# An equivariant 2-to-2 layer whose sums, line terms and slope are placed on other engines, and streaming matmuls placed between the steps of a window attention

## The reference, cut to what matters

```python
diag = jnp.diagonal(x, axis1=-2, axis2=-1)
sum_diag = jnp.sum(diag, axis=-1, keepdims=True)
sum_rows = jnp.sum(x, axis=-1); sum_cols = jnp.sum(x, axis=-2)
sum_all = jnp.sum(sum_rows, axis=-1, keepdims=True)
ops = [diag[..., :, None] * eye, sum_diag[..., None] * eye, sum_rows[..., :, None] * eye, sum_cols[..., :, None] * eye,
       sum_all[..., None] * eye, bt(sum_cols[..., None, :]), bt(sum_rows[..., None, :]), bt(sum_cols[..., :, None]),
       bt(sum_rows[..., :, None]), x, jnp.swapaxes(x, -1, -2), bt(diag[..., :, None]), bt(diag[..., None, :]),
       bt(sum_diag[..., None]), bt(sum_all[..., None])]
```

## Time and profile before

| | us |
|---|---|
| three runs | 975.45, 972.47, 974.67 (median 974.67) |
| profiled execution, its own time | 975.6 |
| its span, first to last instruction | 973.8 |
| mean granted TensorE clock | 0.974 |
| busy: PE, DVE, ACT, POOL | 889.0, 414.4, 446.7, 239.2 |
| 1024 dependent steps of L2 (L927, L950), from about 410 to 897 | 487 |

### The profile page before, as it was taken

How to read it: one execution, slowest core, us unless ns; L and a number is a source line. 1 busy time by engine, 2 the same in 40 slices (tenths; PEclk the granted TensorE clock), 3 DMA queues, 4 the chain that set the end, 5 groups by cost and what they waited for, 6 DMA issues and landing times. The chain is left out here.

```text
span 973.8 us, 15415 instructions
## 1 busy us (share of the span) xinstructions
PE 889.0 (91%) x6191; PEld 518.6 (53%) x6272; DVE 414.4 (43%) x714; ACT 446.7 (46%) x1498; POOL 239.2 (25%) x144
## 2 busy tenths in 40 slices
PE   8778889888989888899999999999999999999887
PEld 5336667767845444344444444455555544554543
DVE  5699999999966753500000000002005400202763
ACT  5777777776636531333333333333333333334641
POOL 4149999998910000300000000000000000000410
PEclk9989999999999996999999999999999999999987
DMA  3110000000000000200000000000000000000000
GB/s 82 23 43 2 1 1 1 1 1 1 1 7 1 1 25 11 83 1 1 1 1 1 1 1 1 1 1 1 1 1 1 1 1 1 1 1 2 1 25 11
DMA packets 10220, 8.30 MB, mean 9 GB/s; under 512 B 7246, under 2 KB 8510, under 8 KB 10052
## 3 DMA queue, kind: packets, MB, share of 16 engines
q1 hardware_dynamic: 10148, 7.31, 3.1%
HBM read 5.47 MB, written 0.26 MB: 6 GB/s over the span
## 5 line engine op out<-in xcount | busy, mean ns | idle before, releaser
L908 PE MATMUL L2p_z<-stream 128*128 128x512 bf16 x880 | 342.2, 390 | 0.0
L950 ACT ACTIVATE L2yx<-L2p_z 32x2 f32<-32x2 f32 x1024 | 165.3, 161 | 323.0 <-PE L2p_z L927 323.0
L927 PEld LDWEIGHTS L2p_z<-L2yx,L2v 64*32 64x32 f32 x2048 | 137.6, 104 | 224.7 <-ACT L2yx L950 218.5
L927 PE MATMUL L2p_z<-L2yx,L2v 64*32 64x2 f32 x2048 | 225.5, 178 | 16.9 <-ACT L2yx L950 15.9
L788 POOL TENSOR_TENSOR hc<-hs,cb 128x1024 f32<-128x1024 f32 x64 | 149.6, 2363 | 4.4 <-DVE hs L729 4.4
L558 PEld LDWEIGHTS p_y<-ident,hc 128*128 128x128 f32 x1024 | 123.2, 192 | 16.5 <-POOL hc L788 9.1
L1641 DVE COPY xn_one<-L2yx 32x512 f32<-32x512 f32 (+1 forms) x2 | 0.8, 384 | 302.7 <-ACT L2yx L950 302.7
L558 PE MATMUL p_y<-ident,hc 128*128 128x128 f32 x1024 | 125.4, 276 | 4.3 <-POOL hc L788 4.3
L1641 POOL COPY xn_one<-L2yx 32x128 f32<-32x128 f32 x1 | 0.3, 284 | 484.2 <-SPq L1984 484.2
L729 DVE TENSOR_TENSOR_SCAN hs<-d_a,p_bb 128x1024 f32<-128x1024 f32 x48 | 109.8, 2287 | 6.2
L908 PEld LDWEIGHTS L2p_z<-stream 128*128 128x128 bf16 x943 | 90.1, 96 | 15.1
(11 more groups left out here) (522 smaller groups left out, 898.2 us busy)
## 6 DMA issues: line engine op xcount, KB each, us to landing
y_l<-in_pick SPq DMA_DIRECT2D x1, 768.0 KB
b_parts<-part SPq DMA_DIRECT2D x6, 128.0 KB, 2.3
c_parts<-part SPq DMA_DIRECT2D x6, 128.0 KB, 2.4
pos<-in_pos SPq DMA_DIRECT2D x1, 512.0 KB, 3.6
ao<-in_at_o SPq DMA_DIRECT2D x1, 512.0 KB, 4.0
L1w<-in_L_w SPq DMA_DIRECT2D x1, 297.0 KB
L3w<-in_L_w SPq DMA_DIRECT2D x1, 297.0 KB
above<-in_x SPq DMA_DIRECT2D x2, 128.0 KB, 3.1
```

The costliest lines, as they stand in the source:

```text
L908: pe.matmul(p_z[:, 1, 0:each], stream[:, 0:128], stream[:, 0:each], start=True, stop=True)
L927: pe.matmul(p_step[:, t % 2], v[:, 0:C], yx[:, NB * t:NB * (t + 1)], start=True, stop=True).then_inc(s("preact"), 1)
L950: act.activation(yx[0:C, NB * (t + 1):NB * (t + 2)], p_step[:, t % 2], ACT.Sigmoid).then_inc(s("state"), 1)
```

## The change

In the equivariant stage a table `esum` (128 tokens x 8 x 98 columns: 32 row indicators, 32 column indicators, 32 diagonal indicators, one for the whole diagonal and one of ones) is loaded as a third DMA. Eight float32 matmuls of `xn_tok` by `esum` give all sums in PSUM, and VectorE copies them to `sums`. The biases enter as a sixth term of the lines. The lines are copied to `rc` by VectorE and ScalarE, and TensorE adds them to the product by identity matmuls whose moving operand is a broadcast of `rc`. Matrix 10 moves behind the lines and is followed by two streaming matmuls. The slope is split: ScalarE writes 0.99 x relu to `positive`, VectorE adds 0.01 of the product to `x` and then `positive`. At the stage's end stand 12 streaming matmuls in place of 17. In the attention, 4 streaming matmuls are placed ahead of `sum_squares`, 2 instead of 1 behind it, and 5, 2, 2 and 1 in the last part, the 5 behind a wait for the last maxima.

```diff
...
@@ -1388,92 +1388,99 @@
     experts("L1", 0)
 
 
+    NSUM = 3 * SIDE + 2
     with ExitStack() as st:
         ew = sb("ew", [R, NBASIS, R], stack=st)
         eb = sb("eb", [R, 2], stack=st)
-        sr = sb("sr", [R, SIDE], stack=st)
-        scl = sb("scl", [R, SIDE], stack=st)
-        dg = sb("dg", [R, SIDE], stack=st)
-        tot = sb("tot", [R, 2], stack=st)
+        esum = sb("esum", [128, T // 128, NSUM], stack=st)
+        sums = sb("sums", [R, NSUM], stack=st)
+        sr, scl, dg = (sums[:, k * SIDE:(k + 1) * SIDE] for k in range(3))
+        sd, sa = (sums[:, 3 * SIDE + k:3 * SIDE + k + 1].broadcast_to([R, SIDE]) for k in range(2))
         rc = sb("rc", [R, 3, SIDE], stack=st)
-        acc = sb("eacc", [R, SIDE, SIDE], stack=st)
-        low = sb("elow", [R, SIDE, SIDE], stack=st)
+        positive = sb("epos", [R, T], stack=st)
+        SLOPE = 0.01
         p_a = ps("e2p_a", [128, T], stack=st)
         p_b = ps("e2p_b", [128, T], stack=st)
         p_c = ps("e2p_c", [128, 2, BANK], stack=st)
         p_r = ps("e2p_r", [128, 2, BANK], stack=st)
+        p_s = p_a[0:R, 0:NSUM]
-        xi = xn[:].rearrange("p (i j) -> p i j", j=SIDE)
         with nc.Block() as block:
             @block.sync
             def _(sp):
                 sp.dma_start(ew[:], io["eq_w"]).then_inc(sig["load_eq"], 16)
                 sp.dma_start(eb[:], io["eq_b"]).then_inc(sig["load_eq"], 16)
-                sp.wait_ge(sig["load_eq"], 32)
+                sp.dma_start(esum[:], io["eq_sum"]).then_inc(sig["load_eq"], 16)
+                sp.wait_ge(sig["load_eq"], 48)
 
             @block.tensor
             def _(pe):
                 norm.pe(pe, 6)
-                pe.wait_ge(sig["load_eq"], 32)
-                norm.wait_out(pe)
+                pe.wait_ge(sig["load_eq"], 48)
+                for j in range(T // 128):
+                    last = pe.matmul(p_s, xn_tok[:, j], esum[:, j], start=(j == 0), stop=(j == T // 128 - 1))
+                last.then_inc(sig["eq_sums"], 1)
                 turned = xn[:].rearrange("p (i j) -> p j i", j=SIDE)
                 half = lambda h: (p_c[h * R:(h + 1) * R, h], 16 * h)
+                norm.wait_out(pe)
                 for h, c in halves():
                     pe.matmul(half(h)[0], ew[:, 9], xn[:, c], start=True, stop=False)
+                pe.wait_ge(sig["eq_sums"], 2)
+                bias = lambda k: eb[:, k:k + 1].broadcast_to([R, SIDE])
+                along = [(ew[:, 8], sr), (ew[:, 7], scl), (ew[:, 11], dg), (ew[:, 13], sd), (ew[:, 14], sa), (ident[0:R, 0:R], bias(0))]
+                diagonal = [(ew[:, 2], sr), (ew[:, 3], scl), (ew[:, 0], dg), (ew[:, 1], sd), (ew[:, 4], sa), (ident[0:R, 0:R], bias(1))]
+                down = [(ew[:, 5], scl), (ew[:, 6], sr), (ew[:, 12], dg)]
+                for n in range(6):
+                    for rows, terms in ((slice(0, R), along), (slice(R, 2 * R), diagonal)):
+                        k, what = terms[n]
+                        pe.matmul(p_r[rows, 0, 0:SIDE], k, what, start=(n == 0), stop=(n == 5))
+                for n, (k, what) in enumerate(down):
+                    last = pe.matmul(p_r[0:R, 0, SIDE:2 * SIDE], k, what, start=(n == 0), stop=(n == 2))
+                last.then_inc(sig["eq_lines"], 1)
                 for h in range(2):
-                    last = pe.matmul(half(h)[0], ew[:, 10], turned[:, 16 * h:16 * h + 16], start=False, stop=True)
+                    pe.matmul(half(h)[0], ew[:, 10], turned[:, 16 * h:16 * h + 16], start=False, stop=False)
+                keep_streaming(pe, norm.dump, 2)
+                pe.wait_ge(sig["eq_lines"], 3)
+                rows_of = lambda h: rc[:, 0, 16 * h:16 * h + 16].rearrange("p (i a) -> p i a", a=1).broadcast_to([R, 16, SIDE])
+                columns = rc[:, 1].rearrange("p (a j) -> p a j", a=1).broadcast_to([R, 16, SIDE])
+                for h in range(2):
+                    pe.matmul(half(h)[0][:, 16 * h:16 * h + 15 * (SIDE + 1) + 1:SIDE + 1], ident[0:R, 0:R], rc[:, 2, 16 * h:16 * h + 16], start=False, stop=False)
+                for h in range(2):
+                    pe.matmul(half(h)[0], ident[0:R, 0:R], rows_of(h), start=False, stop=False)
+                for h in range(2):
+                    last = pe.matmul(half(h)[0], ident[0:R, 0:R], columns, start=False, stop=True)
                 last.then_inc(sig["eq_full"], 1)
-                pe.wait_ge(sig["eq_sums"], 1)
-                sd = tot[:, 0:1].broadcast_to([R, SIDE])
-                sa = tot[:, 1:2].broadcast_to([R, SIDE])
-                along = [(8, sr[:]), (7, scl[:]), (11, dg[:]), (13, sd), (14, sa)]
-                down = [(5, scl[:]), (6, sr[:]), (12, dg[:])]
-                diagonal = [(2, sr[:]), (3, scl[:]), (0, dg[:]), (1, sd), (4, sa)]
-                for n in range(5):
-                    for rows, terms in ((slice(0, R), along), (slice(R, 2 * R), diagonal)):
-                        k, src = terms[n]
-                        last = pe.matmul(p_r[rows, 0, 0:SIDE], ew[:, k], src, start=(n == 0), stop=(n == 4))
-                last.then_inc(sig["eq_lines"], 1)
-                for n, (k, src) in enumerate(down):
-                    last = pe.matmul(p_r[0:R, 1, 0:SIDE], ew[:, k], src, start=(n == 0), stop=(n == 2))
-                last.then_inc(sig["eq_lines"], 1)
-                keep_streaming(pe, norm.dump, 17)
+                keep_streaming(pe, norm.dump, 12)
 
             @block.scalar
             def _(act):
                 norm.act(act)
+                act.wait_ge(sig["eq_lines"], 1)
+                act.copy(rc[:, 2], p_r[R:2 * R, 0, 0:SIDE]).then_inc(sig["eq_lines"], 1)
+                halved = lambda h: (slice(h * BANK, (h + 1) * BANK), p_c[h * R:(h + 1) * R, h])
+                act.wait_ge(sig["eq_full"], 1)
+                for h in (1, 0):
+                    c, out = halved(h)
+                    if h == 0:
+                        act.wait_ge(sig["eq_sums"], 3)
+                    act.activation(positive[:, c], out, ACT.Relu, scale=1.0 - SLOPE).then_inc(sig["eq_full"], 1)
 
             @block.vector
             def _(dve):
                 link = chain(dve, "dve")
                 norm.dve(dve)
-                norm.wait_out(dve)
-                dve.tensor_reduce(scl[:], xn[:].rearrange("p (i j) -> p j i", j=SIDE), AX_X, ALU.add)
-                link(dve.tensor_reduce(sr[:], xi, AX_X, ALU.add))
-                link(dve.tensor_copy(dg[:], xn[:, 0:T:SIDE + 1]))
-                link(dve.tensor_reduce(tot[:, 0:1], dg[:], AX_X, ALU.add))
-                dve.tensor_reduce(tot[:, 1:2], sr[:], AX_X, ALU.add).then_inc(sig["eq_sums"], 1)
+                dve.wait_ge(sig["eq_sums"], 1)
+                dve.tensor_copy(sums[:], p_s).then_inc(sig["eq_sums"], 1)
                 dve.wait_ge(sig["eq_lines"], 1)
-                dve.wait_ge(sig["load_eq"], 32)
-                link(dve.tensor_scalar(rc[:, 0], p_r[0:R, 0, 0:SIDE], eb[:, 0:1], None, ALU.add))
-                dve.wait_ge(sig["eq_full"], 1)
-                along = rc[:, 0].rearrange("p (i a) -> p i a", a=1).broadcast_to([R, SIDE, SIDE])
-                down = rc[:, 1].rearrange("p (a j) -> p a j", a=1).broadcast_to([R, SIDE, SIDE])
-                for h in range(2):
-                    i = slice(16 * h, 16 * h + 16)
-                    dve.tensor_tensor(acc[:, i], p_c[h * R:(h + 1) * R, h].rearrange("p (i j) -> p i j", j=SIDE), along[:, i], ALU.add)
-                link(dve.tensor_scalar(rc[:, 2], p_r[R:2 * R, 0, 0:SIDE], eb[:, 1:2], None, ALU.add))
-                dve.wait_ge(sig["eq_lines"], 2)
-                link(dve.tensor_copy(rc[:, 1], p_r[0:R, 1, 0:SIDE]))
-                link(dve.tensor_tensor(acc[:], acc[:], down, ALU.add))
-                diag = acc[:].rearrange("p i j -> p (i j)")[:, 0:T:SIDE + 1]
-                link(dve.tensor_tensor(diag, diag, rc[:, 2], ALU.add))
-                link(dve.scalar_tensor_tensor(low[:], acc[:], 0.01, acc[:], ALU.mult, ALU.max))
-                dve.tensor_tensor(x[:], x[:], low[:].rearrange("p i j -> p (i j)"), ALU.add)
+                dve.tensor_copy(rc[:, 0:2].rearrange("p k j -> p (k j)"), p_r[0:R, 0, 0:2 * SIDE]).then_inc(sig["eq_lines"], 1)
+                for h, c in halves():
+                    dve.wait_ge(sig["eq_full"], 1 + h)
+                    dve.scalar_tensor_tensor(x[:, c], p_c[h * R:(h + 1) * R, h], SLOPE, x[:, c], ALU.mult, ALU.add).then_inc(sig["eq_sums"], 1)
+                for h, c in reversed(halves()):
+                    dve.wait_ge(sig["eq_sums"], 3 + h)
+                    dve.wait_ge(sig["eq_full"], 3 - h)
+                    dve.tensor_tensor(x[:, c], x[:, c], positive[:, c], ALU.add)
                 unchain(link, "dve")
-
-
-
 
 
 
@@ -2067,8 +2074,9 @@
                             last.then_inc(sig["at_mixed"], 1)
 
                         self.centre_new(pe)
+                        keep_streaming(pe, p_o, 4)
                         self.sum_squares(pe)
-                        keep_streaming(pe, p_o, 1)
```

(11 more changed lines are left out.)

## The result

| | before | changed |
|---|---|---|
| median of 7 runs, us | 974.67 (972.47 to 977.26) | 969.66 (968.12 to 970.58) |
| profiled execution, own time / span | 975.60 / 973.8 | 969.31 / 967.5 |
| mean granted clock in it | 0.974 | 0.983 |

The ratio is 0.9945, with 0.993 to 0.996 as its interval: faster, by 5.0 us at the medians where 3.9 were predicted (970.8). In a second set of twelve executions, `after_again`, it took 969.77 (967.96 to 974.32) beside 973.81, ratio 0.9963 [0.9947, 0.9979], so 4.0 us.

A forecast was written before the change was run, and what follows sets the result against it. The bound was taken to be a chain of dependent instructions over all engines. 975.6 - 1.5 - 1.25 - 2.5 = 970.35, plus 0.4 for falls that stay, gave 970.8 us, range 968.8 to 975.5.

The forecast's parts named there:

- The term of 0.4 for falls that stay: Whole kernel: 0.4 us added to the sum for executions in which one of the clock's falls stays.
- The stage: Equivariant stage: next stage's first transpose at 394.25 instead of 396.12, gain 1.87; 1.5 taken, bounds +1.9 and -0.6.
- Sums: Equivariant stage: 8 float32 matmuls take 1.35 us with the clock up at 383.7, replacing 3.7 us of VectorE reductions.
- Matrix 10 and two streaming: Equivariant stage, behind the lines: matrix 10 takes 1.7 us without its drain, two streaming matmuls 0.43.
- Broadcasts: Equivariant stage, lines added by two pairs of 64x512: lower bound 1.74 us, upper 3.4; 1.74 taken.
- Rival 2: Equivariant stage: the broadcasts are read at matrix 10's rate, +1.6 us, total 972.4; chance 0.12.
- The DMA: Third DMA, 401 KB, ahead of the equivariant stage: lands near 382.8, TensorE wants it at 383.6; hidden, 0.8 us spare.
- Behind the last step: Attention, last step to projection: added streaming keeps the clock, six rounds of 0.90 end at 905.2, 1.25 us earlier.
- The attention's end: Attention's last part: streaming holds the clock, 6.29 us of PE become 3.15, less 0.64 on the path; gain 2.5.
- Rival 3: Attention: its gain goes to another wait, half of 3.75 us lost, total 972.7; chance 0.12.
- Rival 1: Equivariant stage: clock falls at 387.14 under 64x64 tile work; stage ends 2.6 us later, total 974.4; chance 0.22.
- Rival 4: Equivariant stage and attention: experts' low clock not left before the broadcasts; stage 5.4 us later, total 983.5; chance 0.08.

The follow-up runs named there:

- no_mid: Changed kernel without the two streaming matmuls between matrix 10 and the added lines: 973.42 us, ratio 0.9966 to the kernel before.
- slope_dve: Changed kernel with ScalarE's two relu given to VectorE, which does the slope alone: 973.40 us, ratio 0.997 to the kernel before.
- hold_both: Changed kernel with more streaming matmuls both around the attention's score blocks 14 to 16 and in both expert layers: 972.46 us, ratio 0.9998 to the kernel before.
- experts_streams: Changed kernel with 1, 2, 2, 2 and 2 more streaming matmuls in the waits of both expert layers: 976.15 us, ratio 1.0025 to the kernel before.
- att_only: Kernel before, old equivariant stage kept, with only the attention's added streaming matmuls and wait: 974.72 us, ratio 1.0016 to the kernel before.
- no_first: Changed kernel without the added streaming around the sum of squares (0 ahead, 1 behind, as before): 972.11 us, ratio 0.9987 to the kernel before.
- sums_dve: Changed kernel with the sums by VectorE reductions again, the eight sum matmuls left out: 978.13 us, ratio 0.9997 to the kernel before.
- stage_only: Changed kernel with the attention as before (no added streaming or wait), only the equivariant stage changed: 977.74 us, ratio 1.0002 to the kernel before.
- hold_third: Changed kernel with 3 and 5 more streaming matmuls around score blocks 14 to 16, near 918: 971.18 us, ratio 0.9960 to the kernel before.
- no_end_streams: Changed kernel without the 5, 2, 2 and 1 streaming matmuls of the attention's end and their wait: 970.98 us, ratio 0.9973 to the kernel before.
- no_last12: Changed kernel without the 12 streaming matmuls at the equivariant stage's end: 974.46 us, ratio 0.9958 to the kernel before.

## Why the prediction was right, and where it was off

**The total.** Against the profiled execution the sum was 970.35, measured 969.31. The three edited places gave 0.68 less than forecast, and the unchanged code 1.7 more. So the prediction was within 1.2 us partly by luck: an error in it was made good by something outside it. The term of 0.4 for falls that stay is about the 0.35 between the changed kernel's median and its profiled execution, but no run ties those 0.35 us to a fall in the edited places, so that agreement is luck too. The sentence behind it, that with the clock held the kernel comes out alike in all executions, held for the first seven (2.5 us apart) and failed for the next twelve, which lie 6.4 apart.

**A reading that was wrong.** The prediction saw three dips of the clock in the slices of before, 16, 17 and the end. Slice 17 is a 9 in the earlier trace rows; the dips are slices 3, 16 and the end. The windows that it went on to use were read rightly, and nothing in the sum hangs on it.

**The stage, -1.5 taken (1.87 worked), -1.40 measured.** The -1.5 was a choice below the sum worked out. Of what is missing from the 1.87, 0.14 is that the turn back takes 1.85 us to the sums and not 1.71, and the rest is the balance of these:
- *Sums*, 1.35 from clock and columns: 1.57. The clock came up at 382.44, 0.19 behind their start and not 0.1, which accounts for 0.05. The rest is there with the clock up as well: in `after_again` the sums take 1.49. The records come every 0.086 us, where 0.082 had been taken from the transposes by their columns, which is another 0.05; what is left lies at the two ends.
- *Matrix 9* 0.91 for 0.88, *lines* 0.91 for 0.96: right.
- *Matrix 10 and two streaming*, 2.13: 2.46, from 385.64 to 388.10. Of the excess 0.16 is the issue gap shown ahead of a streaming matmul. `no_mid` gives the whole for the two as 0.7, not 0.43. This is the largest mis-sized term of the stage.
- *Broadcasts*, bounded 1.74 to 3.4, taken 1.74: the pairs stand 0.89 apart, and streaming starts 0.96 behind the second. Rival 2 is out. The Trainium skill (SBUF — State Buffer, Door 1: The DMA port swizzle) has a penalty only where a read crosses to a new line; a repeated element doesn't. The trace agrees: 0.89 from start to start for a broadcast pair, where the strided matrix 10 takes 1.74 (`no_mid`, 387.11 to 388.85).
- *Slope*, 2.95: 2.72. `slope_dve` shows that the split is worth 1.34.
- *The DMA*: 0.8 to spare was forecast. It landed 3.7 us behind its issue, some 0.9 ahead of TensorE. That is thin: in `hold_both` and `experts_streams`, where the clock is at 1.00 from the stage's start, TensorE is done with the turn back about 1 us sooner and waits for the table, 0.38 and 0.20 us.

**Behind the last step, -1.25 taken, -1.06 measured.** The rounds are 0.89 for a forecast 0.90. The size was off by where they begin: 899.85 was written, 2.62 us behind the last step's end (897.23 in the profile before), and they begin 2.88 behind it. Nearly all of that is ScalarE, whose first exponential starts 0.21 later behind the step's end than before, with 0.48 us instead of 0.27 ahead of its table load. In `att_only` it starts at 1.56 as before, and there the projection stands at 7.95, which is the forecast's 7.97. Why the table load is later in most variants isn't shown. The 8.2 and 9.4 in the prediction's last part had been counted from a rounded 897; from the instruction's end they are 7.97 and 9.21, and 8.15 was measured. Without the first group the fall is back and costs 1.47 (`no_first`). That streaming keeps the clock up here was the forecast's mechanism, and it held in both profiles of the changed kernel, but not in three of the variants that have it; nothing in the prediction allows for a fall that comes as the four begin.

**The attention's end, -2.5 taken, -2.11 measured.** The clock held at 1.00. The five matmuls ahead of the mixing cost nothing, as that still waits 0.47 for ScalarE and stands 24.77 us behind the projection, where before it was 24.77 too. So the whole 2.11 lies behind the mixing. The other five were put at 0.64 on the path; the remaining 0.39 was not separated. Rival 3 (half of the attention's 3.75 goes to another wait) is out: 3.17 of them are there.

**Rival 1** (the clock falls in the stage) did not come in either profile of the changed kernel, but falls inside the changed stage are real: they are in `sums_dve`, `experts_streams` and `hold_both`, where the stage takes 23.25, 20.66 and 20.82 us instead of 16.7. Its price had been put at 4.1 above the forecast (2.6 later instead of 1.5 earlier), and is 4.0 to 4.1 in the latter two and 6.6 in `sums_dve`, which has VectorE's reductions in it as well. That the price fits is luck in part. In `sums_dve` the fall comes within a wait. In the other two a first fall covers the sums and matrix 9, which the rival left out; their second falls, at 387.69 in `hold_both` and 389.27 in `experts_streams`, come as matrix 10 ends, and are the ones nearest to what the rival describes. The Trainium skill (TensorE: Matmul & The Clock Gate, What's actually happening) has the clock fall behind idleness. The trace of `hold_both` disagrees, as the one before did: PE was busy for 3.37 us of the 3.41 ahead of the fall.

**Rival 4** (the low clock isn't left before the broadcasts) is out as well: the clock was up at 382.44 and stayed at 1.00 to the stage's end.

**What the prediction's method missed.** It priced each fall of one profiled execution and took the sum of those removed. The runs show that this is right within a segment and not to be relied on for a median. `stage_only` and `att_only` have their segments' gains in the profile and none in the median. In both profiles the stretch near 918, in code that no edit touched, takes back 2.8 us, and in `stage_only` the falls of the part that was left do the rest. That this is also what happens at the median is likely and not shown: `att_only`'s profiled execution (973.50) is the third shortest of its twelve, and its span is 3.1 below that of before. Over the executions of one kernel, the time rises by 0.34 us for each microsecond spent at 1.2 GHz (`after_again`; 0.31 for the 35 beside it, 0.36 for `stage_only`; from 0.26 to 0.46 over all sets). With 35.5 us in the changed kernel and 49.1 in the one before, 13.6 us at 0.31 to 0.34 are 4.2 to 4.6 us, which is about the whole difference of 4.0 of that comparison. That is a correlation and not a cause shown: `hold_both`, at 24.8, is slower, and in its profile all of that is in the stage, where two of its four low stretches lie on the chain.

**Open.** Falls between 916 and 922 are in the profiles of `stage_only`, `att_only`, `no_first`, `no_mid` and `experts_streams`, and in none of before, of the changed kernel, or of the other six. What brings them on isn't settled: single profiles can't tell chance from cause here. The length of the experts' stretch goes with no edit that I can name: 17.07 us in before, `stage_only`, `sums_dve`, `no_mid` and `hold_third`, and 10.24 in the changed kernel (twice), `att_only`, `no_first`, `no_end_streams`, `slope_dve` and `no_last12`. `hold_third` shows about what it does: from the stage on its segments are those of the changed kernel to 0.1 us, and its span of 970.0 is 3.6 longer than that of `after_again`. Of this the experts' layer has 2.8 (26.4 against 23.6), and what lies ahead of it, with a longer low stretch and one more, has 0.9.

## What to carry to other kernels

Where TensorE's clock comes and goes, a part's gain is read from its segment and the kernel's from many executions of the whole. Two edits that each measure as nothing alone were worth 0.4 to 0.5 per cent together, and one profile cannot say it. Streaming matmuls pay where a fall would lie on the dependent chain, and not everywhere: twelve behind the stage save 2.1 us in the next, while more of them in the experts cost 6 us at the median, and in the profiles of both variants that have them the stage is 4 us longer by falls inside it. A broadcast operand is read at the pace of a plain one, so a line can be added by a matmul with the identity.

## What the runs showed of the hardware that was not expected

- The granted clock falls under work that keeps PE busy: behind 3.37 of 3.41 us in small tiles (`hold_both`), and for stretches of 17.07 us with PE busy in 16.20.
- Less time at 1.2 GHz is not less time: 24.8 us of it in `hold_both` against 35.5 in the changed kernel, and 2.7 us slower at the median.
- One kernel's executions can fall into two groups whose means lie 8.6 us apart, 969.9 and 978.4 (`stage_only`).
- A broadcast moving operand of 64x512 runs at 0.89 us a pair at full clock, like a plain one (0.91 for matrix 9), and at 1.2 GHz the two pairs stand 1.74 apart (`sums_dve`, 393.17 to 394.91).
- An operand read at a stride of 32 float32 elements hardly depends on TensorE's clock: matrix 10 takes 2.00 us at 2.4 GHz (385.64 to 387.64) and 2.16 at 1.2 (`sums_dve`), its drain included, while a broadcast pair goes from 1.05 to 1.95.
